# Graph attention over a sparse matrix on one core: targets placed in two groups, edge marks on ScalarE

## What is computed

```python
hs = layer_norm(h_source, ln1_scale, ln1_bias)
ht = layer_norm(h_target, ln1_scale, ln1_bias)
...
q = (ht @ Wq + bq).reshape(T, H, HD) / jnp.sqrt(jnp.float32(HD))
k = (hs @ Wk + bk).reshape(S, H, HD)
v = (hs @ Wv + bv).reshape(S, H, HD)
logits = jnp.einsum('thd,shd->hts', q, k)
logits = jnp.where(edge_mask[None] != 0, logits, NEG)
probs = jax.nn.softmax(logits, axis=-1)
ctx = jnp.einsum('hts,shd->thd', probs, v).reshape(T, D)
attn = ctx @ Wo + bo
...
ht = ht + attn
ht = layer_norm(ht, ln2_scale, ln2_bias)
...
ff = jax.nn.gelu(ht @ W1) @ W2
return ht + ff
```

## Time and profile before

| | us |
|---|---|
| median of 3 runs | 369.51 (369.49 to 371.01) |
| the profiled execution | 366.63 |
| its span, first to last instruction | 364.8 |
| first gather issued | 132.75 |
| last gather issued | 289.67 |
| last tile's sum read by DVE | 347.22 |
| busy in the span: PE, DVE, POOL, ACT | 247.2, 233.4, 191.1, 157.8 |

### The profile page before, as it was taken

How to read it: one execution, slowest core, us unless ns; L and a number is a source line. 1 busy time by engine, 2 the same in 40 slices (tenths; PEclk the granted TensorE clock), 3 DMA queues, 4 the chain that set the end, 5 groups by cost and what they waited for, 6 DMA issues and landing times. The chain is left out here.

```text
span 364.8 us, 4184 instructions
## 1 busy us (share of the span) xinstructions
PE 247.2 (68%) x1270; PEld 180.3 (49%) x1270; DVE 233.4 (64%) x648; ACT 157.8 (43%) x263; POOL 191.1 (52%) x209
## 2 busy tenths in 40 slices
PE   0339959897995020325999895879987979679900
PEld 0314413433431010215888785768876967578800
DVE  2613078989489854697798677767878679922110
ACT  0816403698766930002566652646534445223200
POOL 2699704325120037777778878887888712311210
PEclk9999967999999555555999998998999899969965
DMA  7993398999993017776765555555654610000000
GB/s 182 380 386 138 136 320 324 351 417 331 401 353 115 1 51 233 227 204 195 208 199 155 173 139 168 155 158 175 200 153 131 163 34 16 15 0 16 26 24 1
DMA packets 27972, 64.34 MB, mean 176 GB/s; under 512 B 6500, under 2 KB 14950, under 8 KB 25895
## 3 DMA queue, kind: packets, MB, share of 16 engines
q0 software_dynamic: 8368, 29.11, 27.5%
q1 hardware_dynamic: 11792, 25.44, 18.9%
q10 hardware_dynamic: 7782, 9.45, 7.3%
HBM read 53.50 MB, written 12.58 MB: 181 GB/s over the span
## 5 line engine op out<-in xcount | busy, mean ns | idle before, releaser
L610 POOL DMA_INDIRECT arena<-kv_scratch,places x79 | 92.8, 1175 | 22.7 <-issue 22.7
L797 PE MATMUL score<-h_t,w_sb 128*128 128x128 f32 x512 | 70.8, 298 | 7.3 <-ACT h_t L1073 7.2
L797 PEld LDWEIGHTS score<-h_t,w_sb 128*128 128x128 f32 x512 | 66.6, 211 | 10.6 <-ACT h_t L1073 10.6
L709 PE MATMUL bank<-arena 128*128 128x512 f32 x128 | 64.5, 643 | 10.8 <-POOLq L553 5.6
L806 PE MATMUL bank<-w_sb,gelu_t 128*128 128x256 f32 x256 | 58.3, 381 | 0.0
L806 PEld LDWEIGHTS bank<-w_sb,gelu_t 128*128 128x128 f32 x256 | 47.6, 190 | 7.9 <-ACT gelu_t L1049 1.9
L709 PEld LDWEIGHTS bank<-arena 128*128 128x128 f32 x128 | 25.6, 205 | 40.2 <-issue 39.0
L1359 DVE TENSOR_TENSOR arena<-arena,tab 128x1024 f32<-128x1024 f32 (+3 forms) x22 | 24.5, 1113 | 16.9 <-DMA arena<-kv_scratch,places 16.9
L627 POOL DMA_INDIRECT out_dram<-y_out,places x16 | 18.5, 1154 | 28.7 <-ACT y_out L1065 25.9
L606 POOL DMA_INDIRECT tab<-tab_scratch,places x16 | 15.6, 974 | 33.4 <-DVE place_value L1335 28.9
L991 ACT ACTIVATE gelu_t<-arena 128x2048 bf16<-128x2048 bf16 x16 | 30.6, 1910 | 3.8 <-issue 2.3
(11 more groups left out here) (127 smaller groups left out, 378.7 us busy)
## 6 DMA issues: line engine op xcount, KB each, us to landing
arena<-in_adj_dram SPq DMA_DIRECT2D x16, 1024.0 KB, 11.5
kv_scratch<-arena ACTq DMA_DIRECT2D x16, 256.0 KB, 5.5
tab_scratch<-arena ACTq DMA_DIRECT2D x16, 256.0 KB, 4.8
arena<-in_x_dram SPq DMA_DIRECT2D x4, 512.0 KB, 6.6
arena<-in_L_gnn_h_target_dram SPq DMA_DIRECT2D x4, 512.0 KB, 8.8
tab_scratch<-in_x_dram SPq DMA_DIRECT2D x1, 2048.0 KB, 13.8
w_sb<-in_L_gnn_W_dram SPq DMA_DIRECT2D x2, 1024.0 KB, 14.7
arena<-kv_scratch,places POOLq DMA_INDIRECT x79, 3.9
```

What stands on the lines that cost most here:

```text
L610: pool.indirect_dma_start(kv_ring[:, ring_at[m] + j, :], None, kv_dram[:, :], at).then_inc(gathered[m][piece], 16)
L709: mm = pe.matmul(proj_ps[n % 2], h_t[:, s, c % 2, k, i * P:(i + 1) * P], weights[:, k, :], start=(k == 0 and s == 0), stop=(k == DK - 1))
L797: mm = pe.matmul(hid_ps[2 * (n % 2) + half][:, f % 4 * P:(f % 4 + 1) * P], w1_sb[:, k, f * P:(f + 1) * P], h2_t[:, n % 2, k, :], start=(k ...
```

## The change

1. **Two groups.** The targets of the first 1024 rows are sorted first, in seven tiles (2, 3, 3, 4, 5, 5, 7 places); of them the 128 with the most edges are left out and go with the other 1024 in nine tiles (in the order 2, 3, 3, 4, 16, 5, 5, 7, 8). There are 98 gathers instead of 95. Group 2's keys, lists, sort and placing stand in the steps -3 to 3 of the finish; POOL waits for them in step 3 (`PLACED`, `group_ready(1)`).
2. **Order of the front.** Eight units, x ahead of h: x0, h0, x1, x2, h1, x3, h2, h3; the last two use one PSUM bank for projections and one for transposes.
3. **Marks by ACT.** `find_edges` is one activation, Relu(1 - 1e7 * adj), that also sums; `count` is gone. Marks 12 to 15 stand in ACT's steps -3 and -2. From tile 8 there are two buffers for adj, so the load of tile t + 1 is issued behind mark t (t from 9). ACT issues the loads from tile 4 on, and SP the first four, behind the weights.
4. **SP** writes k and v to DRAM; `x` is copied to `tab_scratch` in halves.
5. **Ring and banks.** Group 1's rows use the upper 24 places of the ring of 62; PSUM banks are dealt out anew, the hidden layer has two instead of four.
6. **Planner.** Edge work is spread per group: steps -3 to 4 and 4 to 13. Gathers: 7.5 per step from step 3.

```diff
-    SLOTS = [16, 8, 7, 6, 5, 5, 5, 4, 4, 4, 3, 3, 3, 2, 2, 2]
+
+
+    SLOTS_OF = [[7, 5, 5, 4, 3, 3, 2], [16, 8, 7, 5, 5, 4, 3, 3, 2]]
+    SKIPPED = [1, 0]
+    SLOTS = SLOTS_OF[0] + SLOTS_OF[1]
+    FIRST_TILE = [0, len(SLOTS_OF[0]), TILES]
     CLASSES = [9, 8, 7, 6, 5, 4, 3, 2]
     NCLS = len(CLASSES)
-    ROOM = [P * sum(s >= d for s in SLOTS) for d in CLASSES]
-    ORDER = list(range(TILES - 1, -1, -1))
+    ROOM = [[P * (SKIPPED[g] + sum(s >= d for s in SLOTS_OF[g])) for d in CLASSES] for g in range(2)]
+    ORDER = list(range(FIRST_TILE[1] - 1, -1, -1)) + [15, 14, 13, 12, 7, 11, 10, 9, 8]
     PICKS = 16
     EXT = 2 + PICKS
     COLS = sum(2 + s for s in SLOTS)
-    col_of = [sum(2 + s for s in SLOTS[:i]) for i in range(TILES)]
+    col_of = [sum(2 + s for s in SLOTS[:i]) for i in range(TILES + 1)]
+    COLS_OF = [col_of[FIRST_TILE[g + 1]] - col_of[FIRST_TILE[g]] for g in range(2)]
 
     QUARTERS = 4
     QT = TILES // QUARTERS
...
+    UNITS = [(0, 0), (1, 0), (0, 1), (0, 2), (1, 1), (0, 3), (1, 2), (1, 3)]
+    FIRST_UNITS = 6
...
+        def adj_slot(t):
+            return t % AR if t < EARLY else t % 2
...
+        def edges_of(t):
+            slot = t if t < EARLY else t % 4
+            return (edges_low if slot < 4 else edges_high)[:, slot % 4, :]
...
+        def proj_bank(u, i):
+            return banks[1] if u < FIRST_UNITS and i % 2 else banks[6]
...
+        PLACED = 3
+        edge_work = {step: [] for step in range(-LEAD, TILES + 1)}
+        for g, begin, end in ((0, -LEAD, PLACED + 2), (1, PLACED + 1, TILES - 2)):
+            tiles = range(FIRST_TILE[g], FIRST_TILE[g + 1])
+            stretches = [(KEYS, tiles[0], a, b) for a, b in pieces_of(tiles[0])]
+            for m in tiles:
+                if m + 1 in tiles:
+                    stretches += [(KEYS, m + 1, a, b) for a, b in pieces_of(m + 1)]
+                stretches += [(VALUES, m, a, b) for a, b in pieces_of(m)]
+            all_work, work_done = sum(work_in(w) for w in stretches), 0.0
+            for step in range(begin, end):
+                target = all_work * (step - begin + 1) / (end - begin)
+                while stretches and (any(w[0] == VALUES and w[1] <= step + 2 for w in stretches) or
+                                     work_done + work_in(stretches[0]) / 2 < target):
+                    work_done += work_in(stretches[0])
+                    edge_work[step].append(stretches.pop(0))
 
 
         rows_to_fetch = [(m, j) for m in range(TILES) for j in range(-1, SLOTS[ORDER[m]])]
...
+        fetched_by = {step: (min(ROWS_A, int(FIRST_ROWS + STEP_ROWS * (step + LEAD))) if step < PLACED else
+                             min(len(rows_to_fetch), ROWS_A + int(STEP_ROWS_B * (step - PLACED + 1))))
...
+            load_x(0, 1)
...
+            sp.wait_ge(weights_loaded, 16 * N_WEIGHTS)
             for t in range(AR):
-                load_adj(t)
+                sp.dma_start(adj_tile_of(t), adj[t * P:(t + 1) * P, :]).then_inc(adj_loaded[adj_slot(t)], 16)
...
+            save_kv(0)
+            load_x(0, 3)
+            load_x(1, 2)
+            copy_x(0)
+            save_kv(1)
...
+            save_kv(2)
+            load_x(1, 3)
+            save_kv(3)
+            copy_x(1)
...
+            def group_ready(g):
+
+                pool.wait_ge(places_ready, 3 * (g + 1))
+                pool.wait_ge(x_copied[g], 16)
+                for r in range(CT):
+                    pool.wait_ge(qh_saved[r], 16 * 2 * (g + 1))
+                if g == 0:
+                    pool.wait_ge(kv_read, TILES)
+                    for r in range(CT):
+                        pool.wait_ge(kv_saved[r], 16 * CHUNKS)
+                    pool.wait_ge(mean_saved, 16)
...
+            for u in range(FIRST_UNITS):
+                project(u)
+                if u == 2:
+                    make_keys(0)
+                if u == 4:
+                    make_keys(1)
+                turn_rows(u + 2)
...
+            sum_classes(0)
+            sum_ranks(0)
+            project(FIRST_UNITS + 1, range(2))
+            place(0)
+            project(FIRST_UNITS + 1, range(2, CT))
+            make_keys(2)
...
+                    if lo == 0:
+                        if s == PLACED - 5:
+                            make_keys(3)
+                        if s == PLACED - 3:
+                            sum_classes(1)
+                        if s == PLACED - 1:
+                            place(1)
+                        if s == PLACED + 1:
+                            pe.wait_ge(tally_ready, 1)
+                            pe.transpose(tally_ps[0:1, 0:P], tally_row[:, :], ident[:, :]).then_inc(tally_turned, 1)
                 pe.wait_ge(ff_ready, hi)
...
+            def load_adj(t):
+                if t < TILES:
+                    act.wait_ge(edges_ready, (t - AR if t < EARLY + 2 else t - 2) + 1)
+                    act.dma_start(adj_tile_of(t), adj[t * P:(t + 1) * P, :]).then_inc(adj_loaded[adj_slot(t)], 16)
+
+            def find_edges(t):
+
+                act.wait_ge(adj_loaded[adj_slot(t)], 16 * adj_uses(t))
+                edges_free(act, t)
+                if t == QT:
+                    act.wait_ge(const_ready, 2)
+                act.activation(edges_of(t), adj_tile_of(t), ACT.Relu, bias=1.0, scale=-STEEP,
+                               accum_out=tally[:, 0, t:t + 1]).then_inc(edges_ready, 1)
+                if t >= EARLY + 1:
+                    load_adj(t + 1)
+                elif t in (EARLY - 3, EARLY - 2):
+                    load_adj(t + 3)
+                elif t >= 1 and t - 1 + AR < EARLY:
+                    load_adj(t - 1 + AR)
 
             def load_w(dst, a):
                 act.dma_start(dst, a.rearrange("(k p) n -> p k n", p=P)).then_inc(weights_loaded, 16)
...
+            normalise(7)
+            copy_turned(6)
+            find_edges(8)
+            find_edges(9)
+            copy_turned(7)
+            find_edges(10)
+            for i in range(CT):
+                copy_projected(6, i)
+            save_projected(6)
+            find_edges(11)
             act.wait_ge(const_ready, 6)
             act.wait_ge(mean_projected, 1)
-            act.copy(row_zero[:, D:KV], proj_ps[0][0:1, 0:D]).then_inc(mean_copied, 1)
+            act.copy(row_zero[:, D:KV], mean_ps[0:1, 0:D]).then_inc(mean_copied, 1)
             act.wait_ge(mean_copied, 1)
...
+                    if lo == 0 and s < -1:
+                        find_edges(TILES - 4 if s == -LEAD else TILES - 2)
+                        find_edges(TILES - 3 if s == -LEAD else TILES - 1)
...
+            for u in range(FIRST_UNITS):
+                if u + 3 < len(UNITS):
+                    row_stats(u + 3)
+                    row_moments(u + 3)
+                if u == 5:
+                    for n in range(QK):
+                        pick_bank(1, n)
+                if UNITS[u][0] == 0:
+                    add_bias(u, 0)
+                    add_bias(u, 1)
+                    if u == 5:
+                        split_keys(1)
+                    add_bias(u, 2)
+                    add_bias(u, 3)
...
+            list_edges(1)
+            sort_classes(0)
+            spread_totals(0)
+            sort_ranks(0)
+            keep_places(0)
             for n in range(QK):
-                pick_bank(last, n)
-            split_keys(last)
-            list_edges(last)
...
+                        if s == PLACED - 4:
+                            for n in range(QK):
+                                pick_bank(3, n)
+                            split_keys(3)
+                        if s == PLACED - 3:
+                            list_edges(3)
+                            sort_classes(1)
+                        if s == PLACED - 2:
+                            spread_totals(1)
+                        if s == PLACED - 1:
+                            sort_ranks(1)
+                        if s == PLACED:
+                            keep_places(1)
+                            dve.wait_ge(places_ready, 6)
+                            sum_tally()
+                        if s == PLACED + 2:
+                            set_flag()
                     weigh_edges(edges_now[:len(edges_now) // 2])
```

719 lines of the change are left out of this document (386 added, 333 removed).

## The result

The changed kernel takes 430.02 us (median of four runs, 427.02 to 431.86), the kernel before 369.99: 1.161 times as long (interval 1.153 to 1.169). The profiled execution took 427.02, its span is 425.3 us.

| us | before | forecast | after |
|---|---|---|---|
| T0 | 132.75 | 108 | 115.80 |
| T0 to T1 | | 99 | 100.16 |
| T1 to last y sum | | 179 | 190.41 |
| T0 to last y sum | 214.47 | 278 | 290.57 |
| behind it | 17.6 | 17.6 | 18.9 |

A forecast was written before the change was run, and what follows sets the result against it. Before, the front up to the first gather, then POOL's back-to-back gathers, then TensorE's tail bound the kernel. Forecast: 108 + 99 + 179 + 17.6 = 403.6 us span, given as 406 for a run, range 366 to 428.

The forecast's parts named there:

- T0: Time of the first gather, after projections, marks and the first sort; forecast 108 us, 25 us gained.
- T0 to T1: From the first gather to group 2's first gather, through marks, picks, sort and placing; forecast 99 us.
- T1 to last y sum: From group 2's first gather to the last y sum; forecast 179 us, floor 145, top 190.
- behind it: From the last y sum to the end of the span; 17.6 us, taken unchanged from the kernel before.
- the four steps 10 to 13: Steps whose context TensorE needs in the same step; 14 to 16 us serial, 9.6 overlapped, middle taken: 47 for four.
- TensorE's chain of units in T0: TensorE's projections, turns and keys after unit 0, ending near 37 us; 49.3 us more, so 86.
- y sum 9: Sum of tile 9, after the rsqrt intervals adding to 117 us; forecast 115 us after group 2's first gather.
- mark 10's load ahead of a copy: Late in the front, unit 6's first copy waits behind tile 10's mark, whose load lands at 90 to 98 us.
- the floor of 95.5: Least time from first gather to group 2's first gather; up to 110 for clock and waits, 99 taken.
- Rival A: Close rows don't hold POOL: 150 us from group 2's first gather to last y sum, 376 as a run; chance 0.2.
- Rival B: Group 2's marks, lists and sort hidden under group 1, POOL idle little over 20 us; 350 as a run; chance 0.15.
- what would show it: Signs named beforehand, such as first gather at 103 to 117, POOL idle 40 us or more between gathers 36 and 37.

The follow-up runs named there:

- Experiment 3: Changed kernel with DVE's edge work of steps 10 to 13 standing whole ahead of the y sum; ratio 1.126 to the kernel before.
- Experiment 1: Changed kernel with ScalarE's copies of unit 6's turned rows ahead of the normalisation of unit 7; ratio 1.146 to the kernel before.
- e7: Changed kernel with 10 instead of 7.5 gathers per step from step 3 on; ratio 1.119 to the kernel before.
- c2: Changed kernel with unit 6's copies earlier, adj loads and marks 12, 13 earlier, 10 gathers per step, late edge work ahead of y sums; 386.0 us, ratio 1.046.
- e8: Changed kernel with group 2's sort in one piece ahead of step -1's edge work and four marks ahead of the first exponential; ratio 1.122.
- c7: Changed kernel with group 2's sort in one piece, front edits, edge work spread evenly, whole ahead of y sums from step 10, 16-place tile last; 377.5 us, ratio 1.020.
- e4: Changed kernel with all gathers of steps 6, 7 and 8 issued ahead of the step's rsqrt; ratio 1.150 to the kernel before.
- c4: Five-edit kernel c2 with the 16-place tile last, four marks ahead of the first exponential and group 2's sort one step earlier; ratio 1.062.
- e2: Changed kernel with adj loads of tiles 10 to 15 issued one mark earlier; ratio 1.142 to the kernel before.

## Why the prediction was wrong

The forecast was 406 us with a range to 428; it came to 430. Two steps of the sum failed: the four steps 10 to 13, taken as half overlapped, and TensorE's chain of units in T0, which had no wait for unit 7's rows. The direction, the stages and their order were right: T0 to T1 within 1.2 us (99 and 100.2), the pairs of rsqrts from T1 on (forecast 17.6, 12.7, 14.2, 25.6, 19.4, 13.5, 14.2; measured 18.5, 14.3, 13.4, 26.9, 19.2, 13.9, 14.3), the last two steps (16.6 and 16.6), and y sum 9 at T1 + 112.9 for 115. The 21.7 us that were missing in the span are these terms (0.4 of rounding apart):

- **Steps 10 to 13, 13.9 us.** The prediction had both ends, 14 to 16 a step in series and 9.6 overlapped, and took "the middle, 47 for four". It was 60.9, 15.2 a step: the serial end. The order of the two engines decides this, not a mean: DVE's values of tile s + 2 stand behind y sum s - 1, TensorE's turn of that context ahead of the rest of its pass to y sum s. Of TensorE's pass only the first half of the hidden layer (2.05 us) lies beside DVE's values. Experiment 3 moved the values and won 10.4 us. The low clock behind the wait, 1.5 us a step (3.45 for 1.95), was inside the 9.75 that the prediction took from a row of before, and so in its serial end; the choice of the middle is what failed.
- **T0, 7.8 us.** The step "From there: turn 1.9, unit 1 8.5, turn 1, unit 7, ..." counted TensorE's own work from unit 0 to unit 5. That ScalarE's copies of unit 6 stand behind the normalisation of unit 7, whose rows SP loads only behind its third save (issued at 66.8, landed at 75.1), was not in it: 7.0 us and 2.6 of low clock (3.62 and 2.75 us for what takes 1.88 each), 1.8 more than T0 was late by. What it said of the start held: the third projection waited for the third chunk and ran from 29.1 us (30 forecast). The wait it looked for later, mark 10's load ahead of a copy, didn't come. The copy stood at 97.3, within the 92.7 to 100 given, but because TensorE turned unit 7 late: a right number by luck. Experiment 1 took the 7.0 us away and T0 came 3 to 6 us earlier, so a part of the 7.8 stays open, some of it the scatter of T0.
- **Behind the last y sum, 1.3 us, and T0 to T1, 1.2 us,** less 2.1 at y sum 9. In T0 to T1 two errors met: marks 12 to 15 took 5 us more than counted (loads of 6.8 us beside gathers, not 5.0), and the floor of 95.5 had been raised by 3.5, for the clock and TensorE's waits. At y sum 9 luck helped too: the seven rsqrts add up to 120.4 us, 3 more than forecast, but the last stood 7.4 us behind its y sum, behind gathers of POOL, where 2 had been taken.

Rival A (the close rows don't hold POOL) is out by the trace, in which they held DVE for 29.8 us, and by e7, which took this wait away and had the last gather 33.6 us earlier. Rival B is out: POOL stood still for 43 us ahead of T1, and T1 was T0 + 100. Of "what would show it", the first gather and the last piece waiting for its gather came, and the picks nearly (41.9 us after the first gather, not 38). POOL's idle time did not come as written: between gathers 36 and 37 it is 22 us, not 40, and no single stretch is over 20.7, which was named as a sign of being wrong. Its total of 43 is what was forecast (some 45), but half of it lies behind gather 24: the prediction let all 36 gathers go in 52 us and overlooked that the later ones stand behind rsqrts, and these behind DVE's wait for the last quarter's keys.

The forecast counted T1 as a chain of marks and the work behind the picks, and this held: when the chain was cut by 16 us (c2), T1 followed by 15. What it didn't say is what comes next: DVE's 65 us of work ahead of T1, which only the earlier sort (e8, c7) made less. The repairs of single waits gave 6 to 24 us each (differences of the ratios on 370 us; e4 hardly any) and 43 to 53 together, c4 37, and none reached the kernel before. One rival that nobody named can be ruled out: the hidden layer has two banks instead of four, but the last two steps take 16.6 us in both kernels.

## What to carry to other kernels

When work is split so that a second half is prepared under the first, add up everything that stands ahead of the preparation in the order of the engine that does it: that sum, not the length of the preparation, is when the second half can begin. Where two engines hand each other work in every step, follow one step's chain through both orders and decide whether it is in series; a middle between the ends is no estimate. And a schedule of transfers that is one step ahead is close as soon as an engine that issues them also waits for results of the same step; more transfers per step then move the wait to whatever stands behind them.

## What the runs showed of the hardware

- A load of 1 MB (adj) landed 6.8 us after its issue beside POOL's gathers and 7.8 in experiment 1 (medians of three), 8.7 where two such loads ran at once (e2), against 5.0 alone.
- The issue of a gather (a row of k and v) took 0.95 us (1.25 with the gap) in 62 of 82 cases and up to 2.3 us in the others; before, the mean was 1.175. The longest lie at DVE's products and additions of two f32 tiles, none of the long ones at its picks: two gathers, and what DVE did there, in the changed kernel:

```profile
122.33 0.94 POOL L710 DMA_INDIRECT arena<-kv_scratch,places  x1 [0.30 <-issue]
...
174.43 2.21 POOL L706 DMA_INDIRECT tab<-tab_scratch,places  x1 [0.30 <-issue]
```
```profile
121.06 3.27 DVE L1380 MAX8 cand<-score 128x8 f32<-128x128 f32 x16 [5.56 <-PE score L848]
...
174.34 1.48 DVE L1569 TENSOR_TENSOR arena<-arena,tab 128x1280 f32<-128x1280 f32 x1
```
The Trainium skill, SBUF — State Buffer, "Who interferes with whom", says that a VectorE instruction with two SBUF inputs contends with a GpSimd instruction that reads SBUF; a gather reads its list of rows there, and the rows agree (2.21 beside 0.94 us). No run here took it apart.

- Behind several waits of a few us TensorE ran at its lower clock: 3.62 for 1.88 us (behind 7.0 us of rest, granted clock 0.50 from 82.6 to 86.0), 3.45 for 1.95 (behind 3.3 us, 0.52 from 350.8 to 354.1), 0.61 for 0.39 (behind 4.5 us). Not behind each: in experiment 1 it rested for 2.9 us and the next four matmuls took 1.95 us, at a granted clock of 1.00. In the stage between the groups the clock was 0.72 in the mean.
